# Sums of expert rows in a four-layer transformer kernel: from VectorE's additions to TensorE's products with the identity

## What is computed

```
x = x + jnp.tanh(g_ffn[0]) * _L0_ffn_ref(_layernorm(x), ...)      # out = (y_tok * w).reshape(T, TOP_K, H).sum(axis=1), TOP_K = 8
x = x + jnp.tanh(g_xattn[1]) * _L1_xattn_ref(_layernorm(x), ctx, ...)  # mLSTM: gates, four heads, a norm over each head
x = x + jnp.tanh(g_ffn[1]) * _L1_ffn_ref(_layernorm(x), ...)      # route the top half of the tokens through D -> 1024 -> D
```

## Time and profile before

| what | value |
|---|---|
| median of 3 executions | 2937.91 us (2932.11 to 2945.46) |
| the profiled execution, its own time | 2936.56 us |
| its span, first to last instruction | 2934.8 us |
| TensorE busy | 2482.4 us, 85% |
| VectorE busy | 1826.0 us, 62% |
| ScalarE busy | 1170.2 us, 40% |
| mean granted TensorE clock | 0.922 |

### The profile page before, as it was taken

One profiled execution on the slowest core, in us unless ns is written; L12 is line 12 of the kernel. 1 busy time (PEld: TensorE's weight loads), 2 busy tenths in 40 slices (PEclk: granted clock), 3 DMA queues, 4 the chain that ended last, 5 costly groups with the idle time before them and its releaser, 6 DMA issues. The chain is left out here.

```text
span 2934.8 us, 35618 instructions
## 1 busy us (share of the span) xinstructions
PE 2482.4 (85%) x12608; PEld 1337.2 (46%) x12608; DVE 1826.0 (62%) x4072; ACT 1170.2 (40%) x2095; POOL 755.5 (26%) x462
## 2 busy tenths in 40 slices
PE   6888972966787799899899979989988989997996
PEld 2333331323454444545554635554454555463554
DVE  5667754446877474477667357748447775835774
ACT  1433430312333153356444146535225653514662
POOL 1002352510000041044323024324104432402441
PEclk8999985985888799999999989999999999998998
DMA  7411007994310100244320124440024442012442
GB/s 226 137 37 16 16 15 203 307 294 156 101 46 1 77 1 1 87 114 121 95 74 8 73 69 118 110 122 1 8 88 107 109 108 79 8 57 60 113 124 72
DMA packets 114111, 261.26 MB, mean 89 GB/s; under 512 B 36326, under 2 KB 56422, under 8 KB 107914
## 3 DMA queue, kind: packets, MB, share of 16 engines
q1 hardware_dynamic: 95130, 224.45, 25.6%
q10 hardware_dynamic: 12656, 25.97, 3.5%
q0 software_dynamic: 6144, 8.48, 1.0%
HBM read 121.91 MB, written 31.78 MB: 52 GB/s over the span
## 5 line engine op out<-in xcount | busy, mean ns | idle before, releaser
L858 POOL TENSOR_SCALAR pbuf<-pbuf,recip 128x1024 f32<-128x1024 f32 x128 | 364.4, 2847 | 945.7 <-DVE recip L762 945.7
L807 ACT ACTIVATE pbuf<-ps,least 128x1024 f32<-128x1024 f32 x256 | 284.3, 1113 | 295.7 <-DVE least L755 215.1
L755 DVE CUSTOM_DVE_ANT_0 ps<-ps,spare 128x1024 f32<-128x1024 f32 x256 | 308.0, 1245 | 148.8 <-PE ps L687 148.0
L584 POOL TENSOR_SCALAR pbuf<-pbuf,recip 128x512 f32<-128x512 f32 x128 | 200.4, 1578 | 449.2 <-DVE recip L505 449.2
L712 PE MATMUL ps<-work,vh 128*64 128x256 f32 x2048 | 251.4, 389 | 0.0
L555 ACT ACTIVATE pbuf<-ps,least 128x512 f32<-128x512 f32 x256 | 172.6, 686 | 146.0 <-DVE least L495 146.0
L769 DVE STREAM_TRANSPOSE pbuf<-pbuf 128x2048 f32<-128x2048 f32 (+1 forms) x128 | 226.3, 1768 | 0.0
L1557 ACT ACTIVATE early<-ps 128x1536 f32<-128x1536 f32 x86 | 123.9, 1441 | 200.2 <-PE ps L1372 200.2
L1635 DVE TENSOR_REDUCE mh<-ps 128x3 f32<-128x1536 f32 x86 | 150.0, 1744 | 63.6 <-PE ps L1361 62.8
L712 PEld LDWEIGHTS ps<-work,vh 128*64 128x64 f32 x2048 | 138.1, 138 | 94.3 <-issue 35.5
L447 PE MATMUL ps<-consts,pbuf 128*128 128x128 f32 x1024 | 145.2, 281 | 29.8 <-DVE work L519 25.2
(11 more groups left out here) (383 smaller groups left out, 4175.3 us busy)
## 6 DMA issues: line engine op xcount, KB each, us to landing
work<-pbuf SPq DMA_DIRECT2D x784, 96.0 KB, 2.5
work<-pbuf ACTq DMA_DIRECT2D x240, 96.0 KB, 3.0
early<-in_L_wgu SPq DMA_DIRECT2D x22, 768.0 KB, 15.1
expert_rows<-zero_rows SPq DMA_DIRECT2D x16, 1024.0 KB, 11.5
spare<-expert_rows SPq DMA_DIRECT2D x16, 1024.0 KB, 5.8
early<-in_L_wd SPq DMA_DIRECT2D x22, 384.0 KB, 18.6
arena<-in_L_wo SPq DMA_DIRECT2D x8, 1024.0 KB, 8.0
arena<-in_L_wff SPq DMA_DIRECT2D x4, 2048.0 KB, 9.4
```

Source lines behind the costliest of these rows:

```text
L584: nc.gpsimd.tensor_scalar(x, x, recip[:, n % 8:n % 8 + 1], None, mult).then_inc(probs_ready[1], 1)
L755: nc.vector.tensor_tensor_reduce(out=x, in0=x, in1=mask, scale=1.0, scalar=FMAX, op0=add, op1=ALU.min, accum_out=least[:, n % 8:n % 8 + 1])\
L807: nc.scalar.activation(to, x, ACT.Exp, bias=least[:, n % 8:n % 8 + 1], scale=-1.0, accum_out=sums[:, n % 8:n % 8 + 1]).then_inc(taken, 1)
L858: nc.gpsimd.tensor_scalar(unit(n), unit(n), recip[:, n % 8:n % 8 + 1], None, mult).then_inc(pool_divided, 1)
```

## The change

The four sums of the first batch stay with VectorE. The other twelve (j = 4 to 15) are made by TensorE: eight products of the 128x128 identity with a 128x256 slice of the row tile add up in one PSUM bank, and ScalarE copies the result to `yacc`. The bank is the fourth of a unit: bank 7 for b1 and b3, bank 3 for b2 (SUMS_BANK). TensorE's sum waits until the sum before it has been copied (`row_kept`); the first broadcast of b1 waits until b1's four sums are copied, and output tile 1 of b0 and b1 until those of b2 and b3 are. The copy has a planned time 2 behind that of the sum. The planned times of b2's and b3's sums move from 52 to 122 down to 46 to 110. Loads and the layernorm of b1 to b3 now wait for TensorE's sums (`row_ready`) or ScalarE's copies.

```diff
-    SUMS = ((-9, -6, -3, -0.5), (8, 13.5, 15, 32), (52, 62, 74, 84), (92, 99, 107, 122))
+    SUMS = ((-9, -6, -3, -0.5), (8, 13.5, 15, 32), (46, 56, 66, 76), (82, 91, 100, 110))
+    SUMS_BANK = (None, 7, 3, 7)
...
@@ SyncE
                     if j >= YG:
-                        sp.wait_ge(summed, j - YG + 1)
+                        i = j - YG
+                        sp.wait_ge(*((summed, i + 1) if i < NT else (row_ready, i - NT + 1)))
...
                     if b == 1:
-                        sp.wait_ge(summed, TILES)
+                        sp.wait_ge(row_ready, TILES - NT)
...
@@ TensorE, broadcast(h)
+                        elif b == 1:
+                            pe.wait_ge(row_kept, NT)
...
@@ TensorE, output tile t
+                        if t == 1 and r == 0:
+                            pe.wait_ge(row_kept, NT * (2 + u))
...
+                def row_sums():
+                    for j in range(NT, TILES):
+                        b, t = divmod(j, NT)
+                        yield SUMS[b][t]
+                        pe.wait_ge(y_in[j % YG], 16 * (j // YG + 1))
+                        if b >= PAIR and t == 0:
+                            pe.wait_ge(Ls[SUMS_BANK[b] // 4]["d_ready"], H1)
+                        if j > NT:
+                            pe.wait_ge(row_kept, j - NT)
+                        for k in range(TOPK):
+                            last = nc.tensor.matmul(ps[:, SUMS_BANK[b], 0:D], ident, yg[j % YG][:, k, :], start=k == 0, stop=k == TOPK - 1)
+                        last.then_inc(row_ready, 1)
+
+                side_by_side(*chains(part), row_sums())
...
@@ ScalarE
+                def row_sums():
+                    for j in range(NT, TILES):
+                        b, t = divmod(j, NT)
+                        yield SUMS[b][t] + 2
+                        act.wait_ge(row_ready, j - NT + 1)
+                        if b >= PAIR and t == 0:
+                            act.wait_ge(Ls[b % PAIR]["xn_ready"], 1)
+                        nc.scalar.activation(yaccs[b % PAIR][:, t, :], ps[:, SUMS_BANK[b], 0:D], ACT.Copy).then_inc(row_kept, 1)
+
+                side_by_side(*chains(part), row_sums())
...
@@ VectorE
-                    v.wait_ge(summed, NT * (b + 1))
+                    if b:
+                        v.wait_ge(row_kept, NT * b)
+                    else:
+                        v.wait_ge(summed, NT)
...
                 def row_sums():
-                    for j in range(TILES):
+                    for j in range(NT):
```

More of the change, by code:

```diff
@@ L2202, in layer1 @@
         weights_in, small_in, summed = sem("weights1_in"), sem("small1_in"), sem("B_summed")
+        row_ready, row_kept = sem("B_row_ready"), sem("B_row_kept")
         zero_ready, sum_order, gw_ready = sem("B_zero_ready"), sem("B_sum_order"), sem("B_gw_ready")
@@ L2444, in part @@
                         last.then_inc(L["out_ready"], 1)
-                side_by_side(*chains(part))
+                def row_sums():
[11 more added lines that the diff above has]
+                side_by_side(*chains(part), row_sums())
             @block.scalar
```

## The result

The changed kernel took 2946.92 us (median of 19 executions, 2940.27 to 2957.42), the kernel before, run beside it, 2941.39 (19 executions, 2929.53 to 2952.75). The ratio is 1.0026 with a 95% interval of 1.0014 to 1.0038: about 7.7 us slower (the two medians lie 5.5 us apart), clear of zero, and inside the half per cent that the prediction called no difference. The prediction had 0.5 us faster, a median of 2937, and a range up to 2945, which the median passes.

The account below looks back on a forecast made before the run. The prediction held that no engine bounds the stage alone, VectorE and TensorE alternating as the busier. Its terms, 1.3 + 2.5 - 1.5 - 2.8 = -0.5 us, took the profiled 2936.56 to 2936; predicted median 2937, range 2924 to 2945.

Parts of the forecast that it names:

- stretch 4: From 757 to 837 at the fast clock: TensorE's added sums against VectorE's relief, -2.8 us, ends -5 and 0.
- the walk: Following the three engine queues in four pieces of the stage with the planned times merged; shifts sum to -0.5 us.
- 1, to b0's first broadcast: Sum 4 delays b0's gates, sums 5 and 6 fill TensorE's gap: +1.3 us, ends 0 and +2.6.
- 2, to b1's turn: b0's heads: sum 7 stands in TensorE's queue without idle time, +2.5 us, ends 0 and +3.5.
- 3, to b1's first broadcast: b1's gates to 757: sum 8 delays gates but VectorE's scan comes earlier, -1.5 us, ends -5 and -0.6.
- one of the signs that the prediction named for being wrong: A clock column well over 0.55 before 757; TensorE waiting for row loads was the other.
- The rival of the risen clock: Wide products in TensorE's gaps raise the clock before 757, saving 21 us there; -22 us in all, 2916, chance 0.09.
- the chance of 0.83: Probability given to a near balance, the time staying within 0.5% of the kernel before.
- the gap before the third output tile: TensorE's idle 4.6 us before 794.90, waiting for VectorE's evacuation of the first tile, was to vanish.
- sum 7 as a cost with nothing given back: Behind b0's last broadcast: 3.5 us at clock 0.50 or 1.86 at 1.00, while VectorE's old place frees nothing.
- b2's gate on VectorE: Begins at 815.52 before the change; was to begin at 811.2, after VectorE lost five sums.
- The rival that TensorE's queue is the bound: TensorE's product order sets the end and VectorE's relief gives nothing: +22 us, 2960, chance 0.05.

Follow-up runs that it names:

- four products: Changed kernel with each TensorE sum taking four of its eight products, half of the expert rows left out; stage 343.4 us, ratio 0.9963 to the kernel before.
- the doubled run: Changed kernel with every TensorE sum made twice, the second overwriting the first; stage 400.4 us, ratio 1.0144 to the kernel before.

## Why the prediction was wrong

**The price of a sum.** This is the step that failed. The prediction says that "at clock 1.00, 16 of them with their weight loads took 3.72 us, 0.23 each, so that a sum of eight is 1.86 us". The sixteen were records, and a float32 product is two, so they were eight products and the price of one whole sum was 3.72 us; at 0.50 it would be 7. The twelve sums cost 48.8 us of TensorE (the group by line after, busy us, mean ns | idle before), not 32.2, and the term that carries most of it is that of stretch 4, where the six sums stand in a queue without gaps:

```profile
L2463 PE MATMUL ps<-spare,consts 128*128 128x256 f32 x192 | 48.8, 412 | 0.6 <-ACT yacc L2541 0.6
...
L2541 ACT ACTIVATE yacc<-ps 128x256 f32<-128x256 f32 x12 | 4.6, 384 | 40.0 <-PE ps L2463 40.0
```

Twice 32.2 would be 64.4. The rest is the clock: sums 4 to 9, which I put at 0.50, were at 1.00 for the most part and took 27.0 us and not twice 21.0 (4.12, 3.72 and 3.69 for the first three). The run with half the products has the price that I reckoned with at clock 1.00, 1.9 us for a sum, and it says what the factor of two was worth: 362.1 - 343.4 = 18.7 us of the stage. A count of the source (4 batches x 4 tiles x 8 = 128 products) against the group of line 2442 in the trace of before (256 records) would have shown it.

**The gain was undervalued.** At the reckoned number of records the walk gave -0.5 us, and the run gave -9.3. By stretches, predicted against that run (the third term was meant up to 757, 16 us beyond b1's first broadcast, so that the last two rows compare best as a sum, -4.3 against -7.6 and +4.7):

| stretch | term | four products | changed kernel |
|---|---|---|---|
| 1, to b0's first broadcast | +1.3 | -2.4 | +0.6 |
| 2, to b1's turn | +2.5 | +0.6 | +2.4 |
| 3, to b1's first broadcast | -1.5 | -2.2 | -0.4 |
| 4, the rest | -2.8 | -5.4 | +5.1 |

The first two terms kept TensorE at 0.50, the next two left it nearly so before 757. In truth gates, scores and sums 5 and 6 ran at the upper level; in the changed kernel too the windows after show 0.67 and 0.64 where they had 0.50 and 0.55, which is one of the signs that the prediction named for being wrong. The halved run had this:

```profile
682.00:718.00 36.00, 29.01 (x114) 19.40 (x114) 17.39 (x79) 8.65 (x35) 2.54 (x4) 0.55 0.40 157
718.00:757.00 39.00, 27.76 (x119) 16.98 (x120) 29.00 (x94) 12.01 (x24) 1.27 (x2) 0.71 0.26 82
...
783.00:808.00 25.00, 24.37 (x101) 17.86 (x100) 20.64 (x63) 6.01 (x10) 0.00 (x0) 1.00 0.16 62
808.00:837.00 29.00, 25.78 (x104) 15.15 (x103) 16.67 (x50) 12.39 (x16) 0.00 (x0) 1.00 0.00 1
```

Its twelve sums took 26.9 us of TensorE and not 32.2, and behind 783 the clock was 1.00 where the earlier trace rows had 0.86 and 0.94. So the -9.3 holds VectorE's relief and a higher clock, and no run separates the two. The rival of the risen clock was half right, but not the way that I gave it: the long row of narrow head products stays at the lower level after as before (705.21 above still has 2.07 for a broadcast), and the 21 us that I put on it were not there.

**The two errors had opposite signs.** 18.7 too little cost and some 9 too little gain leave 9.5 us, a size that still rounds to "the same"; that it does is luck. So is the first stretch: sums 4 to 6, at twice the records and twice the clock, took 11.5 us where I had 10.5, and the +0.6 lies within the ends of its term. In the second, sum 7 took 6.12 us for my 3.5, and the +2.4 against +2.5 is a coincidence too. The median lies 2 us beyond the range, while the chance of 0.83 was on the right side. The kernel before, run beside it, had a median of 2941.39, 3.5 us above the one shown at first, and that alone carries more than the 2 us.

**What held.** The hand-over of 0.6 us; ScalarE's copies at 0.384 us, exactly the price of their nearest row; the row loads, for which no sum waited noticeably (0.6 us of idle time before line 2463 in all); the gap before the third output tile, gone; sum 7 as a cost with nothing given back. b1's scan began right behind the logarithm (743.58 after 743.50). **What fell.** Sums 10 to 12 are 11 us and not 5.6, and b0's first output tile came 7.9 us later than by b1's broadcast alone, instead of 3.8. The products of b0's third head came 5.1 us later, less the late start, and not up to 3.5. b2's gate on VectorE, which I had 4.3 us earlier, came 6.8 us later by its distance from the stage's start (823.32 - 641.59 against 815.52 - 640.59). The rival that TensorE's queue is the bound is the one that came nearest behind 757, with 9.5 us of its 22 for the whole stage.

## What to carry to other kernels

Before pricing an operation from a row, match the count of its records with the count in the source; where one instruction of the program is two in the trace, a price for each record is half the price. Work that is moved from a busy engine to a busier one has to be placed in the gaps of the second, and a queue without gaps passes on nearly the whole of it (0.40 us of a product's 0.46 in the doubled run). And first ask whether the work needs to be where it is at all: here sums 12 to 15, made from 798 to 835 us and not wanted before b3's gate at 872.12, stood in the fullest stretch of VectorE's queue. Moving them, and with them sums 10 and 11, with the engine as it was, made the kernel some 13 us faster by the ratio (7.8 by the stage), where changing their engine had made it 7.7 slower (9.5 by the stage).

## What the hardware showed that I hadn't expected

A float32 product of 128x256 is two matmul records here and takes 0.46 us at clock 1.00. In the run with four products the eight records of sum 4 took 2.57 us, the first of them at the lower clock level, and the gates behind them stood at the upper one (1.91 us); in the kernel before, where the turn was followed by 0.69 us of waiting, the same gates took 3.63. How the chip decides on the level is not shown by these runs.

VectorE's instructions of 0.16 to 0.17 us took 1.06 to 2.28 us while GpSimd added 128x1024 values. Later in the same run one sees which are stretched, GpSimd first and then VectorE:

```profile
785.26 4.66 POOL L2324 TENSOR_TENSOR spare<-spare 128x1024 f32<-128x1024 f32 x2
```

```profile
787.67 0.37 DVE L2671 TENSOR_TENSOR ps<-ps,work 128x195 f32<-128x195 f32 x1
788.14 0.16 DVE L2635 TENSOR_TENSOR small<-ps,en 128x4 f32<-128x4 f32 x1
788.34 0.16 DVE L2636 SCALAR_TENSOR_TENSOR small<-ps,small 128x4 f32<-128x4 f32 x1
788.53 1.41 DVE L2637 TENSOR_SCALAR small<-small 128x4 f32<-128x4 f32 x1
```

With one of the two operands in PSUM (`ps`) they keep their time, and so do the one-operand statistics of the layernorm. Of the nine that are stretched in the stage, six read two operands from SBUF and three are TENSOR_SCALAR with a single one (line 113 at 1.06 and 1.10 us, line 2637 at 1.41 instead of 0.17). The Trainium skill (SBUF — State Buffer, "SBUF: two separate sides") says that VectorE and GpSimd share a port pair by an exclusive lock, held for a whole instruction, and that on VectorE's side it concerns operations with two operands in SBUF, while GpSimd reads SBUF, and operations in a mode that uses both ports. This trace agrees as to the first kind, by the six; for the three the second kind would be the reason, but no trace here shows in which mode an instruction ran.
